# Three of the key weight units' low parts move from GpSimd to VectorE in a one-core graph transformer layer

## The reference, cut to what matters

```
xn = layernorm(x)
# GNN: two projections in a row for each of q, k, v, and a mask made from the edges
q = xn @ wq.T + bq;   k = xn @ wk.T + bk;   v = xn @ wv.T + bv
q2 = q @ wiq.T + biq; k2 = k @ wik.T + bik; v2 = v @ wiv.T + biv      # 16 heads of 64
attn = softmax(q2 @ k2.T / 8 + mask)
gnn  = (attn @ v2) @ wo.T + bo
# mix: attention with weights on the rows of the scores
mix  = softmax((q' @ k'.T / 8) * spiky_weights) @ v' @ Wout + bout
x = x + gnn + mix
x = x + softmax(fff_q(ln(x)) @ fff_k(ln(x)).T / 32) @ fff_v(ln(x))
```

## Time and profile before

| what | value |
|---|---|
| median of 3 runs | 807.25 us |
| the profiled execution / its span | 807.75 / 806.0 us |
| PE busy | 766.9 us (95%) |
| DVE busy | 487.9 us (61%) |
| ACT busy | 381.0 us (47%) |
| Pool busy | 182.1 us (23%) |
| low parts of units on DVE (L847) | 58, mean 2349 ns |
| low parts of units on Pool (L364) | 10, mean 4589 ns |
| chain that ended last, by engine | PE 81%, DVE 10%, ACT 7% |

### The profile page before, as it was taken

The page is one execution under the profiler, slowest core; times in us unless marked ns, Lnnn a source line. Parts: engine busy times, 40 slices in busy tenths (PEclk is TensorE's granted clock), DMA queues, the critical chain, the costliest instruction groups (busy, mean ns, idle before and its releaser), DMA issues.

```text
span 806.0 us, 12163 instructions
## 1 busy us (share of the span) xinstructions
PE 766.9 (95%) x4766; PEld 726.0 (90%) x4766; DVE 487.9 (61%) x934; ACT 381.0 (47%) x655; POOL 182.1 (23%) x137
## 2 busy tenths in 40 slices
PE   0899999999999999999999999988999999999998
PEld 0888999998999999999999999877998998999996
DVE  6468874785775677567676776675543454352532
ACT  3453565564655556586867552343333333321420
POOL 6352332322322230260404485000000000000000
PEclk9999999999999999999999999999999999999999
DMA  5222222322223323212121632312332223231202
GB/s 191 104 85 102 69 89 105 106 104 65 94 106 105 105 65 122 106 52 106 53 105 53 235 105 94 135 53 105 118 140 108 105 105 104 105 132 33 98 1 78
DMA packets 14389, 79.59 MB, mean 99 GB/s; under 512 B 3216, under 2 KB 3504, under 8 KB 5616
## 3 DMA queue, kind: packets, MB, share of 16 engines
q1 hardware_dynamic: 11088, 74.45, 25.7%
q0 software_dynamic: 2960, 4.26, 1.6%
q10 hardware_dynamic: 288, 0.14, 0.1%
HBM read 76.66 MB, written 2.19 MB: 98 GB/s over the span
## 4 chain that ended last, share of the span: by engine, by line
PE 81%; DVE 10%; ACT 7%; issue 1%; DMA 1%; DVEq 0%; ACTq 0%
PE g_bank L1391 44%; PE g_bank L1418 13%; PE o_bank L1473 4%; PE t_bank L1462 3%; PE s_bank L1761 2%; DVE w_lo L847 2%; ACT w_hi L489 2%; PE s_bank L1450 2%; PE s_bank L1451 2%; PE s_bank L1349 2%; PE g_bank L1349 2%; ACT q_st L526 1%; PE t_bank L1761 1%; ACT q_st L524 1%; PE g_bank L1850 1%
## 5 line engine op out<-in xcount | busy, mean ns | idle before, releaser
L1391 PE MATMUL g_bank<-act_hi,w_hi 128*128 128x384 f32 x632 | 220.3, 349 | 0.1
L1391 PE MATMUL g_bank<-act_hi,w_lo 128*128 128x384 f32 x632 | 212.0, 335 | 0.0
L1391 PE MATMUL g_bank<-act_lo,w_hi 128*128 128x384 f32 x632 | 211.5, 335 | 0.0
L847 DVE TENSOR_TENSOR w_lo<-raw,w_hi 128x2048 fp32r<-128x2048 f32 x58 | 136.2, 2349 | 36.6 <-ACT w_hi L489 36.0
L489 ACT ACTIVATE w_hi<-raw 128x2048 fp32r<-128x2048 f32 x67 | 127.9, 1908 | 25.0 <-PE s_bank L1761 12.5
L1391 PEld LDWEIGHTS g_bank<-act_hi,w_hi 128*128 128x128 f32 x632 | 119.0, 188 | 3.6 <-issue 3.4
L1391 PEld LDWEIGHTS g_bank<-act_lo,w_hi 128*128 128x128 f32 x632 | 118.9, 188 | 0.0
L1391 PEld LDWEIGHTS g_bank<-act_hi,w_lo 128*128 128x128 f32 x632 | 118.6, 188 | 0.0
L415 POOL DMA_INDIRECT edge_table<-ew,eidx x51 | 69.7, 1366 | 156.5 <-DMA edge_table<-ew,eidx 153.3
L364 POOL TENSOR_TENSOR w_lo<-raw,w_hi 128x2048 fp32r<-128x2048 f32 x10 | 45.9, 4589 | 106.4 <-ACT w_hi L489 106.3
L989 DVE TENSOR_TENSOR pT_lo<-t_bank,pT_hi 128x384 fp32r<-128x384 f32 x96 | 50.4, 551 | 26.2 <-ACT pT_hi L583 25.5
(11 more groups left out here) (252 smaller groups left out, 1570.7 us busy)
## 6 DMA issues: line engine op xcount, KB each, us to landing
raw<-wstream_dram SPq DMA_DIRECT2D x68, 1024.0 KB, 4.8
x_sb<-x_dram SPq DMA_DIRECT2D x3, 512.0 KB, 5.2
y_acc<-x_dram POOLq DMA_DIRECT2D x3, 512.0 KB, 5.3
out_dram<-out_sb SPq DMA_DIRECT2D x6, 256.0 KB, 2.0
edge_table<-ew,eidx POOLq DMA_INDIRECT x51, 2.2
edge_table<-mask POOLq DMA_DIRECT2D x1, 576.0 KB, 4.3
mask<-edge_table POOLq DMA_DIRECT2D x1, 576.0 KB, 4.3
bo_b<-bo_dram POOLq DMA_DIRECT2D x1, 512.0 KB, 7.1
```

The lines of the kernel that those rows point to most:

```text
L847: V.tensor_tensor(flat(w_lo[s][:, :, :]), raw[:, s, :], flat(w_hi[s][:, :, :]), ALU.subtract) \
L1391: last = mm(out, w2[a], x2[b], start=k == 0 and a + b == 0, stop=not after and k == KT - 1 and a == 1)
```

## The change

Units 28, 31 and 34 leave `ON_POOL`. Pool's program loses the three passes on them: the first stood between `split_mix(1)` and `split_mix(2)`, the others each ahead of the pass on the same group's V unit. DVE's program gets them, in groups 0 to 2, behind the last tile of the third head's maxima and ahead of `join(g, 1)`. PE and SP wait for these units on DVE's semaphore in place of Pool's.

```diff
-ON_POOL = (U_K0, U_A0, mix_v(0), U_GNN + 4, U_GNN + 5, U_GNN + 7, U_GNN + 8, U_GNN + 10, U_GNN + 11, U_OUT + 1)
+ON_POOL = (U_K0, U_A0, mix_v(0), U_GNN + 5, U_GNN + 8, U_GNN + 11, U_OUT + 1)
@@ block.gpsimd @@
             split_mix(0)
             split_mix(1)
-            split_lo(U_GNN + 4)
             split_mix(2)
             split_mix(3)
-            for n in (U_GNN + 5, U_GNN + 7, U_GNN + 8, U_GNN + 10, U_GNN + 11):
+            for n in (U_GNN + 5, U_GNN + 8, U_GNN + 11):
                 split_lo(n)
@@ block.vector, GNN groups @@
                 take_pT(tile(1), (2,))
                 maxima("gnn", g, 2, (2,))
+                if more:
+                    split_lo(n + 2)
                 join(g, 1, pv_gnn(g, 1))
                 scale_pair(g, 0)
                 maxima("gnn", g, 3)
```

## The result

The changed kernel's median is 809.06 us (807.99 to 811.22, 20 runs) against 807.63 us (806.88 to 809.69, 20 runs) for the kernel before. The ratio is 1.0015, 95% interval 1.0009 to 1.0022: about 1.2 us slower, inside the 0.2% that the prediction called no difference, but clear of zero. The profiled execution has a span of 808.2 us, 2.2 over the 806.0 of before.

The account below looks back on a forecast made before the run. PE, busy for 95% of the span, was taken as the bound. Terms 0 + 0 + 0.88 on the profiled 807.75 gave 808.63; 0.50 lower for the median gave 808.13, said as 808.1, range 806.8 to 809.5 us.

Parts of the forecast that it names:

- What bounds the kernel: Whole span: PE is busy 95%; Pool's key-unit passes end 3.0 us ahead of need, so making them sooner gains nothing.
- Part 1: Moved key-unit passes on DVE, three groups: 2.29 us each, ending about 0.94 us before PE's need; cost 0.
- Part 2: Unit 30's load, into unit 28's slot, starts at 352.20 instead of 350.10; 9 us of room, cost 0.
- Part 3: Group 0: Pool's early fourth mix piece collides with DVE's pass on unit 27, delaying PE's release by 0.88 us.
- I count the full 0.88: Group 0: the 0.88 us delay of DVE's pass on unit 27 reaches PE whole and stays to the end.
- A: Group 0: early pieces miss DVE's pass, or waits take the delay up; no loss, 807.25 us; chance 0.14.
- B: Key units, three groups: a disturbed moved pass overruns its cover and PE waits; 2.9 us slower, 810.1; chance 0.09.
- C: Three groups: Pool's passes had slowed other engines, so the 0.69 us idle times go; 1.2 us faster, 806.1; chance 0.05.

Follow-up runs that it names:

- Pool held: Changed kernel with Pool again waiting for unit 28's high part ahead of split_mix(2), DVE keeping the moved passes; 807.52 us, ratio 1.0003.
- late variant: Changed kernel with DVE's pass on the key unit behind join and scale_pair instead of ahead of them; 814.68 us, ratio 1.0087.
- Pool's order alone: Kernel before with split_mix(2) and split_mix(3) put ahead of Pool's pass on unit 28, no pass moved to DVE; 809.55 us, ratio 1.0018.
- PE kept busy: Changed kernel with 12 products that nobody reads put into PE's idle time in group 0; 808.94 us, ratio 1.0011.

## Why the prediction was right, and what it missed

The forecast of 808.1 us and a loss of 0.88 had the right sign and cause, and the measured median of 809.06 lies in the range. That it lies as near as it does is in part luck: the half clock that follows the wait was not in the sum, and the timed loss stayed small because the kernel before often loses time to a half clock as well (below). Point by point:

**What bounds the kernel**: right. Pool's passes on key units were nobody's wait; the kernels without them on Pool (changed, and Pool held) gained nothing.

**Part 1, the pass on DVE, cost 0**: right. The pass took 2.29 us and ended at 354.45; the key unit's first product came as it did before, 2.23 us later with all of PE's rows. The late variant measured the cover at 0.91 us where 0.94 was reckoned, and DVE's remaining idle time ahead of Q's second bank is 0.84 where 0.86 was. With Pool held, the three passes together cost nothing measurable, though one of them took 3.17 us and used up all but 0.07 us of the cover.

**Part 2, the transfer, cost 0**: right. Nobody waited for a load in the groups; unit 30's high part came at 368.39, which is 366.14 plus PE's lag of 2.25.

**Part 3, the collision, 0.88**: right in place, cause and size. PE's first idle time grew by 0.87. Both Pool's order alone (the same wait, and a loss of the same size, with no pass moved) and Pool held (no loss with all passes moved) show it.

**The step that was mis-sized** is the sentence "I count the full 0.88", and with it "from there on every PE row 0.9 us later". I took a longer wait to cost its length. In group 0 it cost its length and then 1.56 us more, since PE was granted half its clock for the next eleven products or so: 2.4 us for 0.87. PE's 1.59 us of idle time had left the clock alone, 2.46 us did not, in 4 records of 4 against 0 of 9 for everything shorter. In the two records of PE kept busy the collision was still there and the half clock of group 0 was not, which speaks for the idle time and against the collision as its cause. It is not a proof: all 12 timed runs of that kernel had a half clock somewhere, and ten of them were of a kind that was not recorded.

**Why the timed loss is nearer to 1.2 than to 2.2 us.** The median of the kernel before is a mixture. Of its 35 timed runs, 14 had no half clock (807.24 us), 7 had one stretch (807.40) and 14 more than one (808.94); the changed kernel had one stretch in 29 of 32 (808.92). Against runs of before without a half clock the change thus costs 1.7 us, against those with the most of it nothing. The records point to the normalisation as the place where the kernel before pays: where group 0 has its half clock, the normalisation was spared one in three records of four; elsewhere 6 of 9 had one, at 1.2 to 1.5 us, or 2.25 with PE kept busy. That the changed kernel is repaid there is a fit of counts, not shown. The remaining 0.5 us between 1.7 and 2.2 is a chance of the two recorded executions: that of before took 0.5 us over the median of its kind (807.75), that of the changed kernel 1.0 over its own (809.93), and starts alone differ by up to 2 us between records.

**Rivals.** A (no loss) is out. B (PE waits for key units) did not come; its mechanism is real, as the late variant shows, only its condition failed. C (Pool's passes slow the others) is out: the 0.69 us of idle time is the same with and without Pool beside it, in all three groups.

## What to carry to other kernels

When a pass is taken off an engine's queue, ask first what stood behind it: here Pool's two pieces came 20 us sooner and fell on the one DVE pass that PE waits for, while the moved passes themselves were free. Holding Pool back only moved the collision to a pass with 0.94 us of cover, where it cost nothing. Price a longer wait on TensorE by the granted clock behind it too, not by its length alone. And a wait is better removed than guarded: one ACT instruction moved into a hole won 1.75 us of PE's time and made the collision harmless.

## What the runs showed of the hardware that was not expected

The half clock in the normalisation comes and goes between executions of one and the same kernel: the kernel before had it in one record of three (0.86 of the clock from 540 to 552 us), with products there slow for about 3 us and 1.4 us lost. The idle time there is 2.1 us in every record, and 7 of the 13 records have the half clock. So 2.1 us of idle time was followed by it in some executions and not in others, where 2.46 us in group 0 was followed by it each time.

PE's first products, at 30 to 33 us, likewise start 0.32 us apart for a while and then 0.17, though the granted clock of these windows is given as 1.00, and where that changes differs from record to record: PE's row of 32.83 us in the kernel before lay between 30.87 (pass late) and 32.98 us (PE kept busy) in others. The two places may be tied. Of the five records of before and Pool held, the three whose row of 32.83 us came 1.2 to 1.7 us early are the three with a half clock in the normalisation, and the two whose row came 0 and 0.5 us early have none; most or all of what was won at the start was lost again there. Five records are few, and why it should be so is open.

These two places, some 2 us and 1.2 to 2.25 us, are as large as the effect of the change. This is why single runs of one kernel lie up to 3.3 us apart, and why a median of few runs cannot show a difference of 1.2 us.
